# Attention with its scores made twice: a maximum pass, then a transposed pass that carries the maximum as a 97th row

## The reference, cut to what matters

```
q      = einsum('bld,dhk->blhk', x, Wq)              # 16 heads of 64, x is the layer-normed input
latent = einsum('bld,dc->blc', x, Wkv_down)          # 32 wide
k, v   = latent @ Wk_up, latent @ Wv_up              # per head
attn   = einsum('bqhd,bkhd->bhqk', q, k) / sqrt(64)  # 512 x 512 a head, causal mask
attn   = softmax(where(mask, attn, min))             # over the keys
y      = einsum('bhqk,bkhd->bqhd', attn, v)
out    = einsum('bqhd,hdo->bqo', y, Wout);  x = x + out
```

## Time and profile before

| | |
|---|---|
| median of 3 runs | 3195.47 us (3191.57 to 3209.33) |
| profiled execution | 3213.54 us, span 3211.7 us, mean granted clock 0.884 |
| busy | PE 2635.5 us (82%), PEld 2129.9 (66%), DVE 2033.9 (63%), ACT 1805.4 (56%), POOL 850.9 (26%) |
| attention stage | from the start to about 1232 us |

### The profile page before, as it was taken

One profiled execution on the slowest core, in us unless ns is written; L12 is line 12 of the kernel. 1 busy time (PEld: TensorE's weight loads), 2 busy tenths in 40 slices (PEclk: granted clock), 3 DMA queues, 4 the chain that ended last, 5 costly groups with the idle time before them and its releaser, 6 DMA issues.

```text
span 3211.7 us, 77203 instructions
## 1 busy us (share of the span) xinstructions
PE 2635.5 (82%) x26192; PEld 2129.9 (66%) x26193; DVE 2033.9 (63%) x5025; ACT 1805.4 (56%) x4422; POOL 850.9 (26%) x1042
## 2 busy tenths in 40 slices
PE   3899898988989997986886289999999978868882
PEld 2777777777777776775765166666666657757661
DVE  2767676666766776773554666567666648745555
ACT  2777777777767775552443265555565546524441
POOL 0000000000000003663445232342342316644451
PEclk9999999999999998667998599889899876669996
DMA  5211112111211111112222200000000001112225
GB/s 143 51 41 42 47 46 49 47 47 42 51 42 41 43 39 39 40 41 58 65 67 72 81 2 2 2 2 2 2 2 2 2 2 38 41 46 67 65 68 169
DMA packets 127035, 140.27 MB, mean 44 GB/s; under 512 B 30540, under 2 KB 89041, under 8 KB 126576
## 3 DMA queue, kind: packets, MB, share of 16 engines
q1 hardware_dynamic: 109808, 101.67, 12.4%
q0 software_dynamic: 16896, 34.12, 3.2%
HBM read 45.85 MB, written 40.54 MB: 27 GB/s over the span
## 4 chain that ended last, share of the span: by engine, by line
PE 47%; issue 18%; DVE 15%; ACT 10%; another core or an unknown queue 4%; SPq 3%; DMA 2%; DVEq 1%; POOL 0%; ACTq 0%; POOLq 0%
PE psum L458 5%; PE psum L427 5%; PE psum L493 4%; ACT probs L447 3%; PE psum L1516 3%; DVE state L1719 3%; DVE neg_max L436 2%; SPq L413 2%; PE psum L1138 2%; PE psum L1564 2%; DVE x_sb L1289 2%; PE psum L544 2%; PE psum L1433 2%; PE psum L1114 2%
## 5 line engine op out<-in xcount | busy, mean ns | idle before, releaser
L447 ACT ACTIVATE probs<-psum,neg_max 128x512 f32<-128x512 f32 (+3 forms) x1024 | 538.8, 537 | 247.0 <-DVE neg_max L436 244.9
L436 DVE TENSOR_REDUCE neg_max<-psum 128x1 f32<-128x512 f32 (+3 forms) x1024 | 457.2, 483 | 54.4 <-PE psum L428 24.9
L427 PE MATMUL psum<-ls,qs 96*128 96x512 f32 (+3 forms) x1024 | 381.0, 397 | 116.0 <-ACT probs L447 101.5
L458 PE MATMUL psum<-ident,probs 128*128 128x128 f32 x2560 | 428.1, 283 | 2.8 <-ACT probs L447 0.8
L1251 POOL DMA_INDIRECT y_tok<-yb,xb x272 | 267.3, 983 | 324.3 <-DVE yb L1226 244.4
L427 PEld LDWEIGHTS psum<-ls,qs 96*128 96x128 f32 x1024 | 198.1, 193 | 221.4 <-ACT probs L447 162.7
L325 POOL TENSOR_TENSOR rstd<-var_eps,half_neg 128x4 f32<-128x4 f32 x32 | 39.2, 1224 | 1109.5 <-DVE var_eps L321 1109.5
L477 DVE COPY probs_t<-psum 128x512 f32<-128x512 f32 (+1 forms) x384 | 230.2, 600 | 149.6 <-PE psum L458 142.7
L915 POOL DMA_INDIRECT x_slot<-pay,pos_i x256 | 256.2, 1001 | 135.0 <-issue 77.2
L458 PEld LDWEIGHTS psum<-ident,probs 128*128 128x128 f32 x2560 | 273.6, 144 | 26.4 <-ACT probs_t L473 10.8
L428 PE MATMUL psum<-causal_r,ident_r 128*128 128x128 f32 x1024 | 235.2, 242 | 0.0
(11 more groups left out here) (320 smaller groups left out, 6745.2 us busy)
## 6 DMA issues: line engine op xcount, KB each, us to landing
qs<-q_h SPq DMA_DIRECT2D x512, 64.0 KB, 2.0
xb<-x_slot SPq DMA_DIRECT2D x272, 66.0 KB
qs<-q_l SPq DMA_DIRECT2D x256, 64.0 KB, 2.0
y<-y_tok SPq DMA_DIRECT2D x32, 512.0 KB, 3.6
y_tok<-yb,xb POOLq DMA_INDIRECT x272
x_sb<-in_x SPq DMA_DIRECT2D x16, 256.0 KB, 5.2
x_slot<-pay,pos_i POOLq DMA_INDIRECT x256
out<-x_sb SPq DMA_DIRECT2D x16, 256.0 KB, 2.9
```

The lines of the kernel that those rows point to most:

```text
L427: pe.matmul(o[:, at:at + n], q, ls[par][0:3 * LD, 0:n], start=(at == 0), stop=False, skip_group_check=True)
L436: last = dve.tensor_reduce(neg_max[:, par, h, qt:qt + 1], bank[u % 3][:, at:at + (qt + 1) * P], AX.X, ALU.max, negate=True)
L447: last = act.activation(probs[:, u % 3, c], bank[u % 3][:, c], ACT.Exp, bias=neg_max[:, par, h, qt:qt + 1], accum_out=row_sum[:, par, h, q ...
L458: last = pe.transpose(bank[3 + u % 2][:, c:c + P], probs[:, u % 3, c:c + P], ident[:, :])
```

## The change: what it does

The scores are made twice. The first pass (`scores_tensor`) makes them with queries as rows and without the mask matmul, 20 units ahead (AHEAD). `max_vector` adds a causal tile from SBUF and takes the row maximum in one `tensor_tensor_reduce`, whose elementwise result is written back into the bank. The 16 negated maxima a row of a group are transposed by one PE transpose (`max_turn_tensor`), copied by ACT (`max_copy_scalar`), and one DMA (`max_sync`) lays them as row 96 of `qs`; row 96 of `ls` is 1. The second pass (`keys_tensor`) makes the scores with keys as rows over 97 rows, so that they come out transposed with the maximum taken off. ACT's exp writes straight to `probs_t`, POOL zeroes the masked half of the diagonal blocks (`mask_gpsimd`). The transposes of the probabilities, their copies and the accumulator outputs are gone. The row sums are made by a second set of matmuls with ones as weights (`sums_tensor`), copied, transposed, inverted, widened by POOL, transposed forward and multiplied on. Values and sums of a group are each one whole block on PE (steps 2 and 6). The query columns are interleaved so that a group's queries move by 3 transfers. Layer-norm pieces, projections and output matmuls move to other steps. Some semaphores are merged, also in the constants' set-up of the third stage.

```diff
-                pe.matmul(o[:, at:at + n], q, ls[par][0:3 * LD, 0:n], start=(at == 0), stop=False, skip_group_check=True)
-                last = pe.matmul(o[:, at + qt * P:at + n], ident_r[:, :], causal_r[:, :], start=False, stop=True,
-                                 skip_group_check=True)
+            positive(pe, "s_max", b * UPS + u - 1)
+                last = pe.matmul(o[:, at:at + n], qs[0:KEYS, h, qt * P:(qt + 1) * P], ls[par][0:KEYS, 0:n],
+                                 start=(at == 0), stop=True, skip_group_check=True)
...
-                last = dve.tensor_reduce(neg_max[:, par, h, qt:qt + 1], bank[u % 3][:, at:at + (qt + 1) * P], AX.X,
-                                         ALU.max, negate=True)
+            dve.sem_inc(s["go_dve"], 1)
+                last = dve.tensor_tensor_reduce(out=bank[u % 2][:, at:at + n], in0=bank[u % 2][:, at:at + n], in1=causal[:, L - n:L],
+                                                scale=-1.0, scalar=-MASKED, op0=ALU.add, op1=ALU.min,
+                                                accum_out=neg_max[:, g % 2, j * QT + qt:j * QT + qt + 1])
...
+        def max_turn_tensor(pe, b, g):
+            pe.wait_ge(s["s_max"], b * UPS + (g + 1) * GU)
+            positive(pe, "mx_out", b * G + g)
+            pe.transpose(ln_bank[:, 0:P], neg_max[:, g % 2, :], ident[:, :]).then_inc(s["mx_mm"], 1)
+        def max_copy_scalar(act, b, g):
+            act.activation(max_t[0:HG * QT, :], ln_bank[0:HG * QT, 0:P], ACT.Copy).then_inc(s["mx_out"], 1)
+        def max_sync(sp, b, g):
+            sp.dma_start(qs[KEYS:KEYS + 1, g * HG:(g + 1) * HG, :].bitcast(F32),
+                         max_t[0:HG * QT, :].bitcast(F32)).then_inc(s["mx_dma"], 16)
+        def keys_tensor(pe, b, par, u):
+            o = bank[2 + u % 3]
+            if u % GU == 0:
+                pe.wait_ge(s["mx_dma"], (b * G + h // HG + 1) * 16)
+            positive(pe, "s_exp", b * UPS + u - 2)
+            for kb, at in KEY_TILES[k]:
+                n = L - kb * P
+                last = pe.matmul(o[:, at:at + n], ls[par][0:KEYS + 1, kb * P:(kb + 1) * P], qs[0:KEYS + 1, h, kb * P:L],
+                                 start=(at == 0), stop=True, skip_group_check=True)
...
-                last = act.activation(probs[:, u % 3, c], bank[u % 3][:, c], ACT.Exp,
-                                      bias=neg_max[:, par, h, qt:qt + 1], accum_out=row_sum[:, par, h, qt:qt + 1])
-        def turn_tensor(pe, b, u):
-        def turned_copy(eng, b, u):
+            act.activation(probs_t[:, g % 2, j, UNIT_AT[k]:UNIT_AT[k] + UNIT_COLS[k]], bank[2 + u % 3][:, 0:UNIT_COLS[k]],
+                           ACT.Exp).then_inc(s["s_exp"], 1)
+        def mask_gpsimd(pool, b, u):
+            pool.affine_select(out=blocks_k, in_=blocks_k, compare_op=ALU.is_ge, fill=0.0, base=0, pattern=[[0, n], [1, P]],
+                               channel_multiplier=-1).then_inc(s["p_done"], 1)
...
+        def values_tensor(pe, b, par, g, kb):
+            for j in range(HG):
+                last = pe.matmul(bank[5][j * LD:(j + 1) * LD, kb * P:L], lat_tok[par][:, kb, :], probs_t[:, g % 2, j, c],
+                                 start=(kb == 0), stop=(kb == QT - 1), skip_group_check=True)
+        def sums_tensor(pe, b, g, kb):
+            for j in range(HG):
+                last = pe.matmul(bank[6][j * LD:(j + 1) * LD, kb * P:L], ones_f[:, :], probs_t[:, g % 2, j, c],
+                                 start=(kb == 0), stop=(kb == QT - 1), skip_group_check=True)
...
-            for j in range(HG):
-                for r, part in enumerate((q_h, q_l, q_h)):
-                    sp.dma_start(qs[r * LD:(r + 1) * LD, g * HG + j, :].bitcast(F32),
-                                 part[j * LD:(j + 1) * LD, :].bitcast(F32)).then_inc(s["q_dma"], 16)
+            for r, part in enumerate((q_h, q_l, q_h)):
+                sp.dma_start(qs[r * LD:(r + 1) * LD, g * HG:(g + 1) * HG, :].bitcast(F32),
+                             part[:, :].bitcast(F32)).then_inc(s["q_dma"], 16)
...
+        AHEAD = 20
+        LN_STATS, LN_NORM, LN_TURN = 1, 8, 10
+        PROJ_AT = {(0, 1): A_ITEMS - 1, (1, 0): 0, (1, 2): 1, (1, 7): 2, (2, 7): 3, (3, 7): 4}
+        MAX_AT = 5
+        PV_AT, SUMS_AT = 2, 6
+        INV_AT = 1
...
+                    keys_tensor(pe, b, par, u)
```

522 lines of the change are left out of this document (277 added, 245 removed).

## The result

The changed kernel takes 3239.1 us, median of 4 runs (3232.3 to 3248.4), against 3194.1 for the kernel before (3191.6 to 3209.3): ratio 1.0126, 95% interval 1.0098 to 1.0155. It is slower, by 1.3%; the forecast was 3085. Run once more on another chip, where the kernel before takes 3054, it took 3107: ratio 1.0195 (1.0136 to 1.0254).

A forecast was written before the change was run, and what follows sets the result against it. It took the PE-DVE-ACT ring's latency to bound the kernel (PE 60 us of work in 70.2), afterwards DVE in step with PE. Sixteen sequences at -6.3 us gave -101, the ends -11: 3195 - 112 = 3083, say 3085; range 3045 to 3150.

The forecast's parts named there:

- Bound and PE's work: Attention stage: PE busiest but no engine full; PE's work falls by 10 us only, to 50.5 us a sequence.
- DVE: Row maxima: 0.692 us for 512 columns plus 0.1 for the accumulator; 2.2 us a head against 1.9.
- ACT, POOL, the maxima's transfer: ACT about 34 us a sequence, not the bound; POOL 20; the maxima's transfer has 6 steps, 7.8 us.
- The step of a group: Twelve steps of PE and DVE in lockstep: 14.3 us a group, with 0.15 for handshakes.
- In the steady state worth nothing, because the twelve were hidden.: Query transfers, three for twelve: land in 5.2 us for 256 KB, wanted 8 steps (9 us) later; no gain.
- key projection and its DVE answer 0.6; latent 1.3 in front of the values: Per-sequence extras beside the groups' steps: 0.6 us for key projection and answer, 1.3 for the token-major latent.
- hidden collisions of the fixed lists: Rival: shared bank and DVE waiting for ACT cost 4 us a sequence more, 3150 us; chance 0.07.
- The clock: Attention stage's PE clock: dropping below 0.98 through more PE idling was named as a sign of a wrong forecast.
- The loop's turn: Attention loop's branch: extra cost over unrolled sequences stays at 2.4 us a sequence.
- The ends: Start and end of attention: +7 before the first exp, -11 in the last 20 units, -7 tail; together -11 us.
- Three issues save some 4 us each: Start of attention: two chains of 9.9 us hanging on twelve transfer issues each shorten by some 4 us.
- -6.3 a sequence: Unrolled attention sequence: 63.9 us against 70.2, from 57.2 for four groups plus 3.3, 0.6, 1.3 and 1.5.

The follow-up runs named there:

- e_reduce: Kernel after with the plain negated maximum reduction in place of the instruction with mask and accumulator output: ratio to before 1.0169, loop 75.1 us a sequence.
- second profile: A second profile of the unchanged kernel after; over fourteen sequences a sequence takes 74.4 us, against 75.1 in its first.
- the new order: Kernel after, own maximum: two query projections before values, answered before exp and maximum; layer norm earlier, latent later: 2989.7 us, ratio 0.9796.
- without the loop: Kernel after with mended step order and plain reduction, the attention's loop of six pairs written out: 2932.7 us against 3058.8 before, ratio 0.9604.
- doubled keys: Kernel after with each transposed score matmul issued twice, 8.5 us a sequence of added PE work: ratio 1.0373, loop 79.5.
- fillers: Kernel after with eight extra 512-column matmuls before each wait for a group's queries: ratio 1.0330, loop 78.4.
- the run with both collisions gone: Kernel after with the token-major latent one step later and, from the second sequence, tiny query transfers (output not the reference's): ratio 0.9831, unrolled 64.4 us.
- second candidate: Kernel after with two query projections before values, answered before exp and maximum, layer norm earlier, latent later, plain reduction: ratio 0.9705, loop 65.1.
- the run of before with three: Kernel before with interleaved heads and three 256 KB query transfers a group in place of twelve of 64 KB: 3188.2 us, ratio 0.9961.

## Why the prediction was wrong

**Bound and PE's work: right, as far as the estimate of 49 us against 50.5 reaches.** Values 2.36, sums 2.29 to 2.36 a block against 2.3: at full clock the 32 long column-tiled instructions take no longer than the 80 short ones of before, 2.39.

**DVE: right.** 0.696 for 512 columns (0.692 foretold), 0.571 for 384 (0.56), and with each a second record of 0.141 (0.1). The next maximum starts with that record and not behind it: a row of maxima goes at 0.62 us for 512 columns and 0.48 for 384 from start to start, against 0.62 and 0.47 for the plain reduction (e_reduce). What the read costs is the answer. From the start of a unit to its last record it is 0.76, 0.87 and 0.49 us, where I had 0.75, 0.95 and 0.50 and the plain reduction has 0.69, 0.75 and 0.42. The Trainium skill's rule that an operation with an accumulator output is two instructions (VectorE: DVE Perf Modes, "Two Vector instructions with no wait between them") holds in this trace, 1024 records. The half rate that the Trainium skill gives for the two-tensor form with two fp32 sources in SBUF (Vector Engine (DVE) Microarchitecture Reference, Points that are easy to get wrong) no run here could show; with one source in PSUM the 0.696 is close to the plain reduction's 0.683.

**ACT, POOL, the maxima's transfer: right.** Exp 599 ns, selects 296 and 408, 8 KB landing in 2.0 us by the median, waited for four times, 1.3 us in all. (20 of the 64 took over 3 us, up to 6.9; the six steps hid them.)

**The step of a group: right.** "With 0.15 for handshakes a group is 14.3 us": group 2, which carries of the sequence's own work only the output addition (its step is 0.6 longer than group 3's), takes 14.38, and group 3 without the late transfer 14.16. The sum for the lockstep came out; its terms were not measured one by one.

**The step that failed first: "In the steady state worth nothing, because the twelve were hidden."** The chain of waits, in order of time:
```profile
281.85 0.60 ACT q_h L402
282.47 0.70 DVE q_l L412
283.19 0.56 SPq L423
283.79 0.60 SPq L423
284.44 6.78 DMA qs<-q_h
291.33 0.50 PE psum L435
```
```profile
291.33 0.50 PE L435 MATMUL psum<-ls,qs 96*128 96x512 f32 x1 [1.61 <-DMA qs<-q_h]
```
I let the landing of 2.0 to 5.2 us begin at the projection and wanted it eight steps, 9 us, later. Copy, subtraction and two issues take 2.6 us first; the third transfer, in flight beside the other two, lands 6.8 us after its issue, not 5.2; and PE comes to the first reader 7.9 us after the copy's start, since I counted a mean step and these are mostly short ones. 9.4 against 7.9: PE stands 1.6 us. It does so in two groups of four, and that is 2.4 us an unrolled sequence alone, 2.8 to 3.5 in the loop. The earlier trace rows could not show it: in before the same transfers had room.

**The term mis-sized most: "key projection and its DVE answer 0.6; latent 1.3 in front of the values".** I saw the latent's work and not its wait. It uses the bank that the key projection's answer still holds, two steps after PE had to wait for the layer norm, and behind it in PE's order stand the values. Group 1 takes 9.5 us more than group 2 where I had 0.6 + 1.3 + 1.5 = 3.4; 2.9 of the 6.1 missing are step 1.2's (1.6 of them half clock on the values; against group 3, which has no output addition there, it is 3.5), 1.6 the first step's, where PE waits for the layer norm (2.6 us against 0.5 and the 0.6 forecast), 1.0 the output quarters, which come to 5.9 for the steps 8 to 11 where group 2 has 3.4, and 0.6 the steps 4 and 5. The rival "hidden collisions of the fixed lists", given 0.07 and 4 us a sequence, had the mechanism and half of the size.

**The clock.** I named a clock below 0.98 as what would prove me wrong and gave it no term. It is 0.91 where before's loop has 0.98. Two places show what it costs, since the same work stands in the traces at both levels. The values of group 1 take 3.97 us for 2.36. And step 1 of group 0 takes 3.5 us, all at half clock, in the sequences of after's loop that follow the loop's turn, and 1.7 us at full clock in the unrolled ones (second profile). In the old order such a loss is partly hidden: behind that slower step the wait for the queries at steps 3 and 4 is gone, and group 0 is as long either way (17.4 us). In all, 10 us of a sequence pass at half clock in after's second profile, 8 in the new order and 4 with the plain reduction too, where the loop's clock is 0.93 and 0.96 (0.98 without the loop). No run changes the clock alone, so how much of the missing 8 us a sequence it is I can't say; doubled keys and fillers raised it to 0.94, but with more work than it could give back.

**The loop's turn: "stays at 2.4".** After takes 75.1 in the loop against 71.6, 3.5 more, the run with both collisions gone 4.7, the new order 3.0; writing the loop out took 1.7 to 1.9 us off (before 72.7 to 70.9, candidate 65.1 to 63.4). Two things make it up. At the turn itself the last step takes 4.8 us for 0.6 in after and 3.2 in the new order. And the sequence behind it starts at half clock: in the new order the sequences behind the turn take 67.8 us against 64.9 unrolled, 2.2 of the 2.9 in group 0, whose step 1 is 3.1 us, all at half clock, for 1.7; without the loop it is 1.7 throughout. I had neither. In after five waits on PE, up to 5.0 us, and six on DVE, up to 7.7, stand in the trace with no releaser, where before's longest are 3.0 and 2.8. Why PE stands longer at the turn than before, I have not settled.

**The ends: the tail right, the start not.** The last two steps save 7.9 and 11.8 us (63.2 and 42.8 against 71.1 and 54.6), 20 where I had 18. But the first exponential starts at 85.5 us where it started at 70.6, 15 later and not 7. (My own terms, 10 + 3.5 less two times 4, give 5.5, not 7.) "Three issues save some 4 us each" saved 0.7 and 0.9: ACT's waits of 9.90 us are now
```profile
50.46 8.97 SPq L423 DMA_DIRECT2D qs<-q_h  x2
57.53 0.60 ACT L402 ACTIVATE q_h<-psum 128x512 fp32r<-128x512 f32 x1 [9.20 <-DMA qs<-q_h]
```
It is the same mistake about landing, in the one place where the trace of before could have warned me: there too issue plus landing was what ACT waited for. All scores of the prologue stand behind it.

In sum: -6.3 a sequence became +1.3 unrolled, and the two collisions, removed, give 64.4 for 63.9. That agreement is in part luck. With both removed, group 0 is 0.7 us longer than group 2, where I had 3.3 for layer norm and outputs, and group 1 is 6.4 longer, where I had 3.4: its first step still takes 2.6 us more than group 2's and not 0.6, and the output quarters 2.5 and not 1.5. Two errors of some 3 us cancel.

## What to carry to other kernels

A fixed order that puts long blocks whole between short steps turns every answer that comes a step late into a wait of a microsecond or more on the engine that owns the blocks, so list for every wait in the order which steps lie between question and answer, at their own lengths and not at the mean, and what resource (here a shared bank) makes it a question at all. Time a transfer from the copy that makes its source to the last landing of all that are in flight together. Two such waits in one ring can hide part of each other: over fourteen sequences each fix alone was worth 2.0 to 2.7 us here, both 6.0. And a sum that comes out is no proof of its terms: here two of 3 us were off in opposite directions.

## What the runs showed of the hardware

- Of three transfers of 256 KB between SBUF tensors, issued some 0.6 us apart, the first landed 4.2 us after its issue, the second 5.7, the third 6.9 (medians of after; up to 7.2 in the run of before with three), those of 64 KB issued every 0.62 us in 2.0. The medians in the views mix the first and the third, which carry one name. An 8 KB transfer lands in 1.8 us at the least, and in 4.9 by the median of the second candidate, where it is issued close behind such a group:
```profile
qs<-q_h SPq DMA_DIRECT2D x114, 256.0 KB, 6.1
qs<-q_l SPq DMA_DIRECT2D x57, 256.0 KB, 5.7
qs<-max_t SPq DMA_DIRECT2D x59, 8.0 KB, 4.9
```
- PE's granted clock fell to half on the block behind two waits of 0.96 and 1.64 us some 4 us apart (after, 176 to 186 us), with PE busy 2.36 of the 4 us before the fall.
- A DVE maximum with accumulator output leaves two records, 0.696 and 0.141 us at 512 columns, and the next maximum starts together with the second.
- The kernel before ran at 3194 to 3197 us in the first two comparisons and at 3052 to 3059 on four other chips. The attention stage of after ended at 1286 us on a slower and at 1273 on a faster chip, and what follows it took 1953 and 1827, so most of the difference lies in the stages behind it.
